# A four-layer kernel of convolution, attention, scan and sampling: the last convolution by pairs of batches, and batch 0's attention scores from whole f32 keys

## What is computed

```python
x = x + relu(deform_conv(gn(x)))          # bilinear gather at offsets, 3x3
x = x + neighbourhood_attention(gn(x))    # 4 heads of 8, window 7x7, relative bias
x = x + mamba_three_directions(gn(x))     # selective scans, 64 channels x 16 states
x = x + sampled(gn(x))                    # below
```

```python
off = conv3x3(x, W) + b                    # 32 -> 64 channels, padding SAME
off = off.transpose(0, 3, 1, 2).reshape(-1, 32, 32, 2)     # 128 maps of points (y, x)
c = clip(off + grid, 0, 31)                # where each output point looks
out = bilinear(x as 128 maps, c)           # one map for each batch and channel
```

## Time and profile before

| | us |
|---|---|
| median of 3 runs | 800.01 |
| lowest and highest | 797.45, 803.14 |
| profiled execution, its device time | 799.63 |
| span of the profiled execution | 797.8 |

### The profile page before, as it was taken

The page is one execution under the profiler, slowest core; times in us unless marked ns, Lnnn a source line. Parts: engine busy times, 40 slices in busy tenths (PEclk is TensorE's granted clock), DMA queues, the critical chain, the costliest instruction groups (busy, mean ns, idle before and its releaser), DMA issues.

```text
span 797.8 us, 12457 instructions
## 1 busy us (share of the span) xinstructions
PE 648.7 (81%) x4051; PEld 406.6 (51%) x4051; DVE 677.0 (85%) x955; ACT 531.3 (67%) x657; POOL 455.2 (57%) x285
## 2 busy tenths in 40 slices
PE   7899998579998962676677777767767898999996
PEld 5555546468884310254444454544545643556563
DVE  7899988559975789999899999998999724899996
ACT  2666514559984568677776877777767301999994
POOL 3788863100002066899899999898998601422221
PEclk9999999789999995689987898998988999999999
DMA  2014101551002032000000000000000002100001
GB/s 54 5 16 103 17 2 30 76 105 33 4 3 83 3 87 43 1 0 1 1 1 1 0 1 1 0 1 0 1 1 0 1 1 52 27 0 0 0 0 27
DMA packets 30034, 15.62 MB, mean 20 GB/s; under 512 B 23982, under 2 KB 25902, under 8 KB 29838
## 3 DMA queue, kind: packets, MB, share of 16 engines
q1 hardware_dynamic: 29694, 14.56, 8.8%
q0 software_dynamic: 288, 0.39, 0.3%
HBM read 5.76 MB, written 0.78 MB: 8 GB/s over the span
## 4 chain that ended last, share of the span: by engine, by line
PE 42%; DVE 35%; issue 7%; POOL 5%; ACT 5%; SPq 4%; DVEq 0%; DMA 0%; POOLq 0%; ACTq 0%
PE ps L550 35%; DVE arena L1339 12%; DVE ps L1012 8%; DVE arena L1012 4%; DVE arena L1058 4%; SPq L378 4%; PE ps L975 4%; POOL arena L1728 3%; PE ps L732 3%; DVE ps L1058 2%; POOL x3t L1728 1%; ACT arena L1687 1%; POOL xn L1728 1%; DVE arena L1282 1%; ACT x L1687 1%
## 5 line engine op out<-in xcount | busy, mean ns | idle before, releaser
L550 PE MATMUL ps<-arena 128*64 128x64 f32 (+4 forms) x1992 | 344.4, 342 | 111.1 <-DVE arena L1339 37.7
L550 PEld LDWEIGHTS ps<-arena 128*64 128x64 f32 (+4 forms) x1992 | 141.8, 142 | 227.8 <-issue 81.5
L1728 POOL TENSOR_TENSOR arena<-arena 128x1024 f32<-128x1024 f32 x81 | 188.2, 2335 | 24.1 <-DVE arena L1339 8.6
L1339 DVE TENSOR_TENSOR_SCAN arena<-arena,ps 128x1024 f32<-128x1024 f32 x66 | 150.9, 2287 | 8.6
L1012 DVE TENSOR_TENSOR ps<-arena,ps 128x1024 f32<-128x1024 f32 x75 | 90.9, 1212 | 7.7 <-PE ps L550 6.9
L1713 ACT ACTIVATE arena<-ps,nycol 128x1024 f32<-128x1024 f32 x64 | 70.5, 1101 | 36.2 <-PE ps L550 36.2
L1674 ACT ACTIVATE arena<-arena,a_col 128x1024 f32<-128x1024 f32 x66 | 75.4, 1142 | 17.1 <-DVE arena L1339 16.8
L1847 POOL TENSOR_TENSOR arena<-arena,bmask 128x128 f32<-128x128 f32 x64 | 30.2, 472 | 84.6 <-PE ps L550 76.0
L1571 ACT ACTIVATE arena<-arena 128x256 f32<-128x256 f32 x128 | 60.8, 503 | 22.3 <-DVE arena L1220 17.8
L1339 DVE TENSOR_TENSOR_SCAN arena<-ps,arena 128x1024 f32<-128x1024 f32 x30 | 68.2, 2272 | 2.7 <-POOL arena L1728 2.6
L550 PE MATMUL ps<-ident,arena 128*128 128x128 f32 x416 | 63.7, 305 | 2.0 <-POOL arena L1728 2.0
...
## 6 DMA issues: line engine op xcount, KB each, us to landing
...
arena<-arena SPq DMA_DIRECT2D x12, 128.0 KB, 3.3
...
```

The costliest lines, as they stand in the source:

```text
L550: return pe.matmul(o, l, r, start=start, stop=stop, **k)
L1339: ve.tensor_tensor_scan(hs_ring[n % RING], decay, add, 0.0, ALU.mult, ALU.add).then_inc(S("scan"), 1)
L1728: return gp.tensor_tensor(o, a, b, ALU.mult)
```

## The change

Two parts of the kernel are rewritten.

**Attention, batch 0.** All 32 units of batch 0 use the f32 form. ACT writes two more masked copies of the keys: `k_own[3]` into `x3t`, and after the value products (`v` at 5, since they read `xn`) `k_own[2]` into `xn`. Batch 0 is no longer moved, neither by SP nor by POOL; SP goes through batches 1, 2 and 3, and PE waits directly on the DMA's semaphores. PE waits for the new keys at group 4.

**Last layer.** The halves of the work are now pairs of batches, p = 0 and 1. A product of pair p has its two batches in 64 partitions, and the other 64 partitions hold the same image shifted by one column, so that one product does two taps of a row (`w_taps[:, 0]`); the third tap is a product with 64 rows (`w_taps[rows_, 1]`, `native`). That makes 12 products for a pair (6 with 64 rows, then 6 with 128), 24 in all. The shifted copies are made by two DMAs on SP (64 rows of 4,620 bytes each), the second issued when the first has landed; `xrow` is copied likewise on ACT's queue. Pair 0's output lies in banks 0 and 1, pair 1's in 6 and 7. `normalize` writes the two images with two operations, and there are two transposes of 64 partitions. PE enters the loop after the first pair's coordinates, and waits for the second's at the first `turn4`. The transposes of `x3t` come before the convolution, between two shorter runs of `keep_busy` (5 and 4), into banks 2 and 3; ACT copies them to `x3_row`. The subtraction that ends the kernel is split: POOL does pair 0's part after its last `stationary`, DVE pair 1's from SBUF. Stores are by batch: SP stores batches 0 and 1 in one DMA each (128 KB) and batch 2 in two, ACT stores batch 3 in two.

Beside these: POOL clears only the 768 columns of `w_conv` that `w_taps` uses; the weights come in 8 DMAs instead of 4; the grid comes as a ready tile `c_point` of 512 points for each partition; several semaphores are merged under one name.

```diff
-        q_own, k_own = x1, [x0, grid_x]
+        q_own, k_own = x1, [x0, grid_x, xn, x3t]
 ...  (SP)
-            for b in range(B):
-                if b >= 2:
-                    eng.wait_ge(s_ld[f"qk{b % 2}"], QK_LOADS - (0 if b % 2 else QK_POOL))
-                    if b == 3:
-                        eng.sem_inc(S("qk_rows"), 1)
+            for b in range(1, B):
+                if b == 3:
+                    eng.wait_ge(s_ld["qk1"], QK_LOADS)
 ...
+            eng.wait_ge(S("gn"), 3)
+            eng.dma_start(flat_image[0][DI:P, 0:WP * WP - 1], flat_image[0][0:DI, 1:WP * WP]).then_inc(s_ld["image"], 16)
+            eng.wait_ge(S("gn"), 4)
+            eng.wait_ge(s_ld["image"], 16)
+            eng.dma_start(flat_image[1][0:DI, 1:WP * WP], flat_image[1][DI:P, 0:WP * WP - 1]).then_inc(s_ld["image"], 16)
 ...
+            eng.wait_ge(S("yout_first"), 2)
+            for b in range(2):
+                store(eng, b, slice(0, NBLK))
             for h in range(2):
                 eng.wait_ge(S("yout"), h + 1)
-                for k in range(4 * h, 4 * h + 4):
-                    eng.dma_start(out.rearrange("b h w c -> (h w) b c")[P * k:P * k + P], yout[:, k]).then_inc(S("stored"), 16)
+                store(eng, 2, slice(4 * h, 4 * h + 4))
 ...  (PE)
-                        if g < OWN // GROUP:
-                            last = mm(o, q_own[:, queries], k_own[h][:, keys])
+                        if b == 0:
+                            last = mm(o, q_own[:, queries], k_own[2 * m + h][:, keys])
 ...
-                if g == OWN // GROUP:
-                    pe.wait_ge(s_ld["qk0"], QK_LOADS - QK_POOL)
-                    pe.wait_ge(s_ld["qk_pool"], QK_POOL)
+                if g == GPB // 2:
+                    pe.wait_ge(S("k_heads"), 2)
                 if g and g < NGROUP and g % GPB == 0:
-                    pe.wait_ge(S("qk_rows"), above(g // GPB))
+                    b = g // GPB
+                    pe.wait_ge(s_ld[f"qk{b % 2}"], QK_LOADS * (2 if b == 3 else 1))
 ...
-            keep_busy(6, 13)
+            keep_busy(6, 5)
+            pe.wait_ge(S("x3t"), 2)
+            for c in range(NBLK):
+                last = pe.transpose(ps[:, 2 + c // 4, P * (c % 4):P * (c % 4) + P], x3t[:, P * c:P * c + P], ident[:])
+            last.then_inc(S("x3_turned"), 1)
+            keep_busy(6, 4)
+            pe.wait_ge(s_ld["conv"], 16 * 8)
+            for p in range(PAIRS):
+                rows_, bank = slice(DI * p, DI * p + DI), 6 * p
+                pe.wait_ge(S("gn"), 3 + p)
+                for ky in range(3):
+                    for h in range(2):
+                        mm(ps[:, bank + h, :], w_taps[rows_, 1, ky], native(p, ky + 16 * h, 2), start=(ky == 0), stop=False)
+                pe.wait_ge(s_ld["image"], 16 * (p + 1))
+                for ky in range(3):
+                    for h in range(2):
+                        last = mm(ps[:, bank + h, :], w_taps[:, 0, ky], image[p][:, ky + 16 * h:ky + 16 * h + 16, 0:C],
+                                  start=False, stop=(ky == 2))
                 last.then_inc(S("conv"), 1)
             pe.wait_ge(s_ld["rows0"], 16 * 6)
             pe.wait_ge(s_ld["b4"], B4_LOADS)
-            pe.wait_ge(S("coord"), 2)
+            pe.wait_ge(S("coord"), 1)
+            pe.wait_ge(S("x3_row"), 1)
 ...
+                        if first and t == LAG_POS:
+                            pe.wait_ge(S("coord"), 2)
 ...  (DVE, normalize)
+                if into is None:
+                    for p in range(PAIRS):
+                        r = slice(DI * p, DI * p + DI)
+                        ve.tensor_scalar(image[p][r, 1:1 + C, 1 - p:1 - p + C], x[r].rearrange("p (h w) -> p h w", w=C),
+                                         small[r, 20:21], small[r, 24:25], ALU.subtract, ALU.mult).then_inc(S("gn"), 1)
+                    return
 ...  (ACT)
+            ac.activation(k_own[3][:], bank2(2), ACT.Identity, bias=sees_bias[:, 3:4], scale=sees[:, 3:4]).then_inc(S("k_heads"), 1)
+            ac.wait_ge(S("v"), 5)
+            ac.activation(k_own[2][:], bank2(2), ACT.Identity, bias=sees_bias[:, 2:3], scale=sees[:, 2:3]).then_inc(S("k_heads"), 1)
 ...
+            ac.wait_ge(S("x3_turned"), 1)
+            ac.activation(x3_row, bank2(2), ACT.Copy).then_inc(S("x3_row"), 1)
+            ac.wait_ge(S("xrow"), 1)
+            ac.dma_start(xrow[0][DI:P], xrow[0][0:DI]).then_inc(s_ld["xrow"], 16)
 ...  (POOL)
-            gp.memset(xpad, 0.0).then_inc(S("xpad_cleared"), 1)
+            gp.memset(image[0], 0.0)
+            gp.memset(image[1], 0.0).then_inc(S("cleared"), 1)
 ...
+            gp.wait_ge(S("x3_row"), 1)
+            gp.wait_ge(S("summed"), above(CPER * NT))
+            for h in range(2):
+                finish(gp, 0, h).then_inc(S("yout_first"), 1)
```

165 lines of the change are left out of this document (85 added, 80 removed).

## The result

| | before | after |
|---|---|---|
| median, us | 799.82 | 778.06 |
| lowest and highest | 797.45, 803.14 | 777.7, 778.75 |
| span of the profiled execution | 797.8 | 776.9 |

The ratio is 0.973 (95% interval 0.970 to 0.976): 21.8 us less by the medians, 20.9 by the spans. The forecast was 776.8, with a range of 772 to 786.

A forecast was written before the change was run, and what follows sets the result against it. No engine is full; the limit differs by layer. Gains of 8.7 (attention), 11.1 (loop entry), 0.2 (transposes gone) and 3.2 (end) make 23.2: span 797.8 to 774.6, with 1.8 around it 776.4, median 776.8; range 772 to 786.

The forecast's parts named there:

- Attention, 8.7 us: Up to group 10's scores: 16.9 us of lost time removed, 7.8 of f32 scores and 0.4 added; 8.7 gained.
- rival 2: Attention: f32 scores of two heads don't overlap between transposes and values; 10.3 us more, 787; chance 0.07.
- the 16.9 us: Attention: time lost in PE's two waits and the slow stretches behind them, all of which can go.
- the second stall: Attention: PE's 4.29 us wait until SP's queue raises batch 1's signal, which sits behind 18 of batch 2's moves.
- Between: Scan layer and its preparation: same scan code, a change of nothing, though it need not run the same to the microsecond.
- rival 4: Scan layer drifts because it starts with another state of the clock; 788; chance 0.05.
- The convolution: Last layer: 0.86 us for each product; pair 0 ends 12 products after the start, pair 1 at 661.7; copies hidden.
- rival 1: Clock falls before the convolution, its pause holding 8 transposes and 9 idle products instead of 13; 779; chance 0.10.
- rival 3: Last layer: shifted copies are late, 1.2 us for the first, and the clock falls; 780 to 781; chance 0.07.
- rival 5: Last layer: shifted copies are cut into pieces of an element, about 75 us each; about 920; chance 0.03.
- The entry: Last layer's loop: PE enters 12.7 us earlier, but POOL's split holds the third `sample`, so the steady part gains 11.1.
- The end: DVE's last additions to the span's end: half the elements for DVE, stores on two queues; 3.2 us gained.

The follow-up runs named there:

- attention alone: The kernel before with only the change of batch 0's attention: 789.98 us, ratio 0.988.
- the last layer alone: The kernel after with attention as before, so only the last layer is changed: 788.58 us, ratio 0.984.
- the kernel with alternating products: The kernel after, with the convolution's 64-row products of the two pairs alternating, then each pair's 128-row products: 777.45 us, ratio 0.973.

## Why the prediction was right, step by step

**Attention, 8.7 us.** Measured to group 10: 8.7, with groups of 3.83 and 2.54 as worked out. The f32 scores of two heads overlap with transposes and values between them (rival 2 falls). One thing about the step was wrong, and it did not touch the price, since the 16.9 us were counted from the trace whatever their cause. The forecast called the second stall a matter of SP's signal alone ("<-SPq L496"). Without that signal only 2.5 of the 7.3 us came back, as PE stood still a little later instead, by my reading for its instructions: in the trace of the kernel before, too, no q8 packet starts between 157 and 169.25, and PE goes on at 170.19. That the change recovers the whole 16.9 I put down to its taking 18 of the 72 moves away, which no run tests by itself. In the kernel after the packets come at 148.5, 160.75 and 166.0, the second still late (a block lasts about 8.4 us in batch 0, worked out from 6.5 us at 96 instructions in 2.54 against 112 in 3.83), but not so late that PE ran dry. And 1.4 us more were gained up to the first scan (10.1 instead of 8.7). That is luck: it compares a profile of before in which the clock falls at the end of attention (0.50 from 246 to 248) with one of after in which it doesn't. Like with like it is 7.8 to 8.3 or 8.9 to 9.5 (above), on both sides of the forecast.

**Between.** "Nothing, though it need not run the same" was right in kind and too small in size: 2.2 us given back, and the same code ranged over 6 us (321.3 to 327.3) in the kernels of this study, with the clock anywhere from 0.50 to 1.00 in windows of five us towards its end. The time at half speed alone doesn't order them: the mean granted clock of the stretch is 0.85 with attention alone (321.28 us) and with the last layer alone (327.20). What makes the difference stays open. It is rival 4 in small. The four kernels with the old attention alone scatter by 4.9 us (322.3 to 327.2), so it needs no change to come about; at 6 us it is the largest uncertainty of the sum, over a quarter of the saving.

**The convolution.** 24 products at 0.86 were to take 20.6 and took 21.43 to the last one's end. The issue was 0.43 for each instruction, with 64 rows or 128, as taken. Missing in the sum were about 0.2 us for each of the three changes between 64 and 128 rows: PE's weight loads are 0.43 apart elsewhere and 0.94 there.

```profile
637.12 0.19 PEld L572 LDWEIGHTS ps<-arena,w_conv 64*128 64x128 f32 x1 [0.24 <-issue]
637.55 0.19 PEld L572 LDWEIGHTS ps<-arena,w_conv 64*128 64x128 f32 x1 [0.24 <-issue]
638.49 0.30 PEld L572 LDWEIGHTS ps<-arena,w_conv 128*128 128x128 f32 x2 [0.76 <-issue]
```

The clock stayed at 1.00, and the copies landed in 3.1 and 4.3 us (4.1 forecast, bounds 3.3 to 6.3): hidden. Rivals 1, 3 and 5 fall.

**The entry.** The step said that PE's entry would gain 12.7 and the third `sample` 11.1, as POOL's split comes next. Measured 11.51 and 10.42. At the entry the term that was too small is the move: the forecast had one issue of 0.6 and 3.3 to land behind DVE's third part, and it took 5.1 (the third part is two moves, so SP's last issue ended 1.3 later, and landed in 3.8); 0.2 more came from pair 0's convolution. At the third `sample` it is the convolution: DVE took pair 1 at +21.47 where the forecast had +20.95. From there POOL's start (2.28) and its split (6.70) came as forecast. That POOL is the one that binds is in the row (1.64 us at the third `sample`) and in the kernel with alternating products, where the wait is gone. What the forecast did not look at is the reverse side: beside POOL's split DVE's factors take 1.06 and 1.60 instead of 0.42. It cost nothing new, since it was so in the kernel before, whose rows at the same place are:

```profile
676.82 1.27 DVE L1407 TENSOR_SCALAR arena<-arena 128x512 f32<-128x512 f32 x1 [2.40 <-ACT arena L1713]
...
680.30 1.23 DVE L1407 TENSOR_SCALAR arena<-arena 128x512 f32<-128x512 f32 x1
```

**The end.** 3.2 forecast, 3.06 measured. The 0.2 for the transposes that are gone did not show; instead DVE's last factor took 0.97 beside POOL's subtraction (768.22, above), and the stretch was 0.5 longer. Moving that subtraction gave it back, and with it the 0.2: 3.43 us from the last `sample` to the last additions, against 3.60 before. So the term that the forecast had at nothing is POOL's new operation beside DVE's last factor.

**The sum.** 8.7 + 11.1 + 0.2 + 3.2 = 23.2 was forecast. By the landmarks it is 10.1 (attention to the first scan) - 2.2 (scan layer) + 10.4 (to the third `sample`) - 0.5 (loop) + 3.1 (end) = 20.9. But for the cause of the second stall the mechanisms were right; the terms that missed were +1.4, -2.2, -0.7, -0.7 and -0.1. The first two don't come from the change and cancel for the most part, which is luck; the three others are misses of the working.
